# Two reorderings on TensorE and a split of the first loads over two issuing engines, in a two-layer decoder kernel

## The reference

```python
x = _layernorm(x + _L0_attn_ref(x, W_in, b_in, W_out, b_out))       # block A
x = _layernorm(x + _L0_xattn_ref(x, ctx_2048, W_fc, ..., W_v, b_v)) # block B
x = _layernorm(x + _L0_ffn_ref(x, ...))                             # block C: 64 experts
...                                                                 # blocks D, E, F: layer 1
# A, for each sequence and 16 heads of 16 features, causal:
weights = softmax(q @ k.T * 0.25 + mask); attn = weights @ v; out = attn @ W_out.T + b_out
# B: sup = relu(ctx @ W_fc.T + b_fc); ref = relu(x @ W_fc.T + b_fc)
# q from ref, k from sup, weights = softmax(q @ k.T * 0.25); result = ref + (weights @ sup) by W_v + b_v
```

## Time and profile before

| what | us |
|---|---|
| median of three runs | 1002.47 |
| lowest and highest | 1000.71, 1004.54 |
| the profiled execution's own time | 1001.67 |
| its span, first to last instruction | 999.9 |
| first matmul | 6.23 |
| one step of the pipeline in A, 51.17 to 60.50 | 9.33 |
| one step in B, 132.46 to 142.37 | 9.91 |

### The profile page before, as it was taken

The page is one execution under the profiler, slowest core; times in us unless marked ns, Lnnn a source line. Parts: engine busy times, 40 slices in busy tenths (PEclk is TensorE's granted clock), DMA queues, the critical chain, the costliest instruction groups (busy, mean ns, idle before and its releaser), DMA issues. The chain is left out here.

```text
span 999.9 us, 18709 instructions
## 1 busy us (share of the span) xinstructions
PE 955.7 (96%) x6121; PEld 755.5 (76%) x6121; DVE 636.5 (64%) x1474; ACT 443.4 (44%) x862; POOL 313.3 (31%) x514
## 2 busy tenths in 40 slices
PE   6999999999999999999999999998999998999994
PEld 4788887687888888888887855667787775888883
DVE  3676777655555555555556666778778865555555
ACT  3777786432332233222222223426776784323321
POOL 1133123244444444444445303210000106344430
PEclk9999999999999999999999999999999999999998
DMA  8000000256433333333333000011111121554501
GB/s 289 13 17 18 2 2 1 51 158 184 142 130 127 111 111 110 111 113 111 111 112 103 21 1 10 1 37 40 27 36 35 34 67 23 127 152 110 113 18 42
DMA packets 37423, 75.55 MB, mean 76 GB/s; under 512 B 7121, under 2 KB 18365, under 8 KB 37222
## 3 DMA queue, kind: packets, MB, share of 16 engines
q1 hardware_dynamic: 37074, 74.53, 25.9%
q0 software_dynamic: 288, 0.23, 0.2%
HBM read 67.57 MB, written 2.40 MB: 70 GB/s over the span
## 5 line engine op out<-in xcount | busy, mean ns | idle before, releaser
L1054 PE MATMUL ps<-shared 128*128 128x512 f32 x1560 | 378.0, 391 | 1.0 <-POOL shared L2105 0.9
L1054 PEld LDWEIGHTS ps<-shared 128*128 128x128 f32 x1560 | 292.0, 188 | 66.6 <-issue 5.1
L1477 ACT ACTIVATE shared<-pT 128x512 fp32r<-128x512 f32 x130 | 82.4, 634 | 287.9 <-DVE pT L1903 287.8
L2103 POOL CAST shared<-wraw 128x512 fp32r<-128x512 f32 (+1 forms) x130 | 91.9, 707 | 295.0 <-PE ps L1080 274.2
L1906 DVE TENSOR_TENSOR al<-pT,shared 128x512 fp32r<-128x512 f32 x130 | 120.8, 929 | 91.0 <-ACT shared L1477 91.0
L1895 DVE TENSOR_TENSOR e<-e,ps 128x512 f32<-128x512 f32 x130 | 89.4, 688 | 122.3 <-PE ps L1054 119.7
L1080 PE MATMUL ps<-shared 128*128 128x512 f32 x520 | 161.9, 392 | 0.3 <-DVE al L1906 0.2
L2105 POOL TENSOR_TENSOR shared<-wraw,shared 128x512 fp32r<-128x512 f32 (+1 forms) x130 | 133.9, 1030 | 10.4
L1080 PEld LDWEIGHTS ps<-shared 128*128 128x128 f32 x520 | 97.4, 188 | 22.5 <-DVE al L1906 1.2
L1471 ACT ACTIVATE e<-ps 128x512 f32<-128x512 f32 x130 | 77.8, 598 | 76.8 <-PE ps L1054 76.8
L1903 DVE TENSOR_TENSOR pT<-e,kbd 128x512 f32<-128x512 f32 x130 | 101.0, 777 | 7.1
(11 more groups left out here) (228 smaller groups left out, 1381.7 us busy)
## 6 DMA issues: line engine op xcount, KB each, us to landing
kbd<-combine_C SPq DMA_DIRECT2D x46, 512.0 KB
wraw<-in_C_w SPq DMA_DIRECT2D x48, 384.0 KB, 8.5
kbd<-combine_F SPq DMA_DIRECT2D x15, 512.0 KB
wraw<-in_F_w SPq DMA_DIRECT2D x17, 384.0 KB, 6.9
kbd<-kbd SPq DMA_DIRECT2D x96, 32.0 KB, 1.9
kT<-kbd SPq DMA_DIRECT2D x48, 32.0 KB, 1.8
c_ctx_t<-in_ctx_t SPq DMA_DIRECT2D x1, 1024.0 KB, 8.8
out<-c_x_rows SPq DMA_DIRECT2D x2, 512.0 KB, 2.9
```

Source lines behind the costliest of these rows:

```text
L1054: mm = pe.matmul(GU[t][s], w[u][:, (c * 2 + s) * P:(c * 2 + s + 1) * P], xx[:, c, t * HALF:(t + 1) * HALF], start=(i == 0), stop=(i == 5))
L1477: act.activation(ah[t][:, :], a2[t], ACT.Copy).then_inc(S("ah"), 1)
L2103: pool.tensor_copy(wh[u][:, lo:hi], wraw[k][:, lo:hi]).then_inc(S("m_wh"), 1)
```

## The change

Three edits. In TensorE's pipeline `ref_rows(t-4)` moves ahead of `project_keys(t-1)`, and `second_transposes(t-2, 1)` moves ahead of `out_T(t-3)`. Of the loads of groups A0, A1 and A2 the nine small ones (tensors with fewer than 256 elements in a row, and the two biases `bv` and `bo` of 256) are issued by ScalarE at its start; SyncE issues the six others, in the old order, and then goes on as before.

```diff
+        SECOND = [t for g in ("A0", "A1", "A2") for t, src in loads[g] if np.prod(src.shape[1:]) < D]
+        SECOND += [W["A", "bv"], W["A", "bo"]]
+
+        def first_loads(eng, queue):
+            for group in ("A0", "A1", "A2"):
+                for t, src in loads[group]:
+                    if queue == any(t is x for x in SECOND):
+                        eng.dma_start(t[tuple(slice(None) for _ in t.shape)], src).then_inc(S(f"{group}_loaded"), 16)
...
-            for group in ("A0", "A1", "A2", "A3"):
-                load_weights(group)
+            first_loads(sp, 0)
+            load_weights("A3")
...
             for t in range(2 * B + 5):
+                if ly == "B":
+                    ref_rows(t - 4)
                 if lp:
                     project_keys(t - 1)
                 if ly == "A":
                     out_project(t - 4)
-                if ly == "B":
-                    ref_rows(t - 4)
...
                 if lx:
                     x_T(t - 5)
+                if lv:
+                    second_transposes(t - 2, 1)
                 if lo == "A":
                     out_T(t - 3)
-                if lv:
-                    second_transposes(t - 2, 1)
...
+            first_loads(act, 1)
             loaded(act, "A0")
```

## The result

The changed kernel took 1005.46 us (median of 15 runs, 1004.72 to 1009.28), the kernel before 1003.6 beside it (15 runs, the three shown ahead of the prediction among them). The ratio is 1.0032, 95% interval 1.0023 to 1.0041, which is 3.2 us of 1003. The means differ by 3.0 us. The two medians differ by only 1.9, because eight of the fifteen runs before lie between 1003.6 and 1004.5 and the others are spread down to 999.4. I count the change as slower by about 3.2 us: a difference clear of the noise, inside the 0.5% that the prediction called "same", and 0.5 us above the upper end of its range.

The account below looks back on a forecast made before the run. TensorE, busy 96%, was taken to bound the kernel. Loads -1.2, `ref_rows` +1.4 and `out_T` 0 turned the profiled 1001.67 into 1001.9 us, or the median 1002.47 into 1002.7, range 1000.6 to 1005.0.

Parts of the forecast that it names:

- What bounds the kernel: Whole span: TensorE, busy 96%, sets the end; its waits are at the start and at the steps in B.
- Part 2: Steps 12 to 16, `ref_rows` ahead of the keys: each 0.26 to 0.33 us longer, +1.4 us taken.
- Part 1: First loads split over SyncE and ScalarE: the start and all behind it 1.2 us earlier.
- A0 is complete at 5.0, which is 1.2 us earlier: Start: `wk` lands at 4.6 and `bk` at 5.0, so the first matmul leaves 6.23 by 1.2 us.
- A2 and the later groups are also issued earlier [...] No one behind them waits longer than before: Loads behind the first group: SyncE saves nine issues, some 4 us, and no later reader waits longer.
- The bound that the long rows might end at a fixed moment: First matmuls: if TensorE's long rows end at a fixed moment, up to 0.6 us of the gain is lost.
- The table load: ScalarE's start: wanted at 7.2 instead of 8.38, with its nine issues done by 5.2, a cover of 2 us.
- The third rival: Start: ScalarE still issuing loads when the first keys are ready; +3.5 us, +4.9 in all, 1007.4; chance 0.05.
- The first rival: Start gains nothing, by interleaving or another last transfer; +1.4 us in all, 1003.9; chance 0.17.
- Part 3: Steps 3 to 10, `out_T` behind the last transposes: same work in another order, cost 0.
- The cover that I named: Steps 3 to 10: ScalarE's 0.21 us idle and about 0.1 overlap absorb a 0.3 us delay; without it 0.8.
- The sum: Whole kernel: -1.2 + 1.4 + 0 on the profiled 1001.67 gives 1001.9; the median becomes 1002.7.

Follow-up runs that it names:

- part 2 alone: Kernel before with only `ref_rows` moved ahead of the keys, run twice (x2, x11): ratios 1.0020 and 1.0023.
- x8: Kernel before with the small first loads split to ScalarE, except `bo`, which SyncE issues ahead of `wo`: 1000.6 us, ratio 0.9991.
- x10: Kernel before with the load split, `bo` still last on ScalarE but in its own semaphore group awaited only by its reader: 1003.2 us, ratio 1.0003.
- x1: Kernel before with only the split of the first loads over SyncE and ScalarE: 1004.5 us, ratio 1.0013.
- x17: Kernel before with only the split of the first loads, second time: 1003.4 us, ratio 1.0014.
- x2: Kernel before with only `ref_rows` moved ahead of the keys: 1004.5 us, ratio 1.0020.
- x11: Kernel before with only `ref_rows` moved ahead of the keys, second time: 1004.2 us, ratio 1.0023.
- x3: Kernel before with only `out_T` moved behind the last transposes: 1001.9 us, ratio 1.0000.
- x12: Kernel before with three extra transposes, results overwritten, in each of steps 12 to 16: 1004.3 us, ratio 1.0026.
- x13: Kernel before with six extra transposes, results overwritten, in each of steps 12 to 16: 1006.0 us, ratio 1.0038.
- x0: Unchanged copy of the kernel before: 1001.5 us, ratio 0.9989.
- x9: Changed kernel with all three edits, but `bo` issued by SyncE: 1004.3 us, ratio 1.0019.
- x4: Kernel before with the load split and the `out_T` move, without the `ref_rows` move: 1005.2 us, ratio 1.0036, six runs.
- x5: The changed kernel with all three edits, run again: 1004.9 us, ratio 1.0039.
- after: The changed kernel with all three edits, in its first measurement and profile: 1005.46 us, ratio 1.0032.
- x15: Kernel before with the load split and the `ref_rows` move, without the `out_T` move: 1005.6 us, ratio 1.0035.
- x14: Kernel before with the `ref_rows` move and three extra transposes in each of steps 12 to 16: 1005.5 us, ratio 1.0028.

## Why the prediction was wrong, point by point

**What bounds the kernel** was right: nearly all that mattered was on TensorE at the two places that the rows had shown, with 0.28 us more at 602.6.

**Part 2 was right, step by step.** The copy into `XT` ends at 112.38, the weight load of `ref_rows` starts 0.10 us later, the keys 0.17 behind it and the values 1.10 behind these, nearly as forecast. A step takes 122.69 - 112.48 = 10.21 against 9.91, so +0.30, and the five make 1.46 to 1.49, against 1.4. The time of part 2 alone came out above that, at 2.0 and 2.3 us. See below.

**Part 1 failed, and it is the step that made the prediction wrong.** Of its terms:

- *"A0 is complete at 5.0, which is 1.2 us earlier"*: mis-sized, and mostly because of its starting point. The 6.23 of the earlier trace rows is the latest first matmul of nine profiles in which SyncE issues all; the others are 5.43 to 6.04, the mean 5.81. With the split (eleven profiles) it is 5.31 to 6.10, the mean 5.64. The gain is 0.2 us, not 1.2. `bk` came as forecast: 1.16 + 3.5 = 4.7. But `wk`, which I had landing at 4.6 by its old 3.0 us, takes 3.6 to 4.4 beside the transfers that ScalarE starts, where it takes 2.5 to 3.0 when SyncE issues all, and now it ends the wait.
- *"A2 and the later groups are also issued earlier [...] No one behind them waits longer than before"*: wrong. I looked at the issues and not at what they collide with. SyncE has six issues instead of fifteen ahead of A3, so A3's 768 KB transfers go out from 4.14 us instead of 8.42 and are under way together with ScalarE's small ones. `bo`, the last of these, lands at 4.82 + 8.1 = 12.9. Before, it was issued at 7.47 and took 3.0: 10.5. It is issued 2.65 us earlier and lands 2.4 us later. All of A2 counts for whoever waits for it, so the first scores start 0.05 to 0.63 us later behind the first matmul than in the kernel before. That the bulk makes `bo` late, and not ScalarE's queue as such, is argued from x8, where SyncE issues it ahead of the bulk and it takes 5.2; no run held the bulk back with `bo` last on ScalarE. It can't be the whole of it: the identity on ScalarE still takes 6.2 us in x8.
- The bound that the long rows might end at a fixed moment: in the nine unsplit profiles the clock's first rise came at 9.25 to 16.02 us of the span, which is 3.7 to 10.0 us behind the first matmul. It is fixed neither in the span nor behind the start, so what a start 0.2 us earlier gives back to it can't be read from one profile.
- The table load was not late (7.89, forecast 7.2; before 8.38), and ScalarE was through with its issues at 5.65 (forecast 5.2). The third rival is out: its issues took 0.39 to 0.94 us each.

Together: after step 2 the ledgers of the eight profiles with `bo` last on ScalarE stand at +0.1 in the mean, those of the nine unsplit ones at -0.7 and those of x8 to x10 at -0.6. So by the ledgers the split costs 0.8 us by then instead of gaining 1.2, and another 0.28 us at 602.6; 1.1 to 1.3 us is what the times of x1 and x17 say. Without the wait for `bo` the times of the split are those of the kernel before (x8, x10). The 0.8 holds the wait of 0.3 us and the later clock, and four of the eight profiles make it.

The first rival had the transfers interleave and the start gain nothing. It was the nearest, but it stopped at zero and could not become a loss. The Trainium skill (DMA: Bandwidth & Descriptors, section "Issuing engines are not separate DMA queues") says that transfers of several issuing engines interleave on the same DMA engines. The landing times of `bo` (8.1 against 3.0) and of the identity (6.7 against 2.2) agree, and go further than the zero that I had worked out from it.

**Part 3**: forecast 0, measured 1.0000 in time and about +0.2 us in the ledgers, 0.03 in each step. The cover that I named nearly holds.

**The sum** was -1.2 + 1.4 + 0 = +0.2. By the experiments it is +1.2 (x1, x17) + 2.1 (x2, x11) + 0 (x3) = +3.3, against 3.2 measured. 2.4 us of the miss are part 1 and 0.7 part 2. Each of these terms is uncertain by some 1 us, so how well the sum closes is in part luck.

**What stays open** is the 0.5 to 0.9 us by which part 2, and x12 and x13, cost more than their ledgers across the five steps, if it is more than noise. The clock is the only thing in the traces that I found to hold them: mean 0.9912 and 0.9919 in x2 and x11, where the kernel before had 0.9925 and 0.9929 beside them. An estimate supports it. One slope fitted to all executions of x0 to x17 and of the kernel before beside them gives 0.62 us for each 0.001 of mean clock; at equal clock x2 and x11 are then 1.2 and 1.7 us above the kernel before, 1.45 in the mean, against 1.47 in the ledgers. It is rough: it leaves 1.9 for x12 (ledger 1.64) and 4.0 for x13 (3.27), and puts x0 at -1.0. The stretch at C is a candidate for the lower clock. It isn't a matter of how late C starts, since it is there at 182.4 and 183.6 and absent at 182.8, 183.6 and 184.4 (x2, x9; x4, x13, x5). But take how far C's first matmul is behind the clock's first rise in the same execution. In five profiles this is 168.3 to 168.9 us (after, x2, x9, x11, x15), and all five have the stretch. Of the other fifteen fourteen have none, at 165.8 to 168.1 or at 169.5 and above; x17, at 164.9, has one and doesn't fit (its first rise, at 18.09 us, is the latest of all twenty). Of the ten profiles without part 2 or more work eight lie at 164.9 to 167.4. So a delay of 1.5 us would push many executions into those 168.3 to 168.9, and one of 3.1 us beyond them, as x14's did (169.5). That fits all but one profile, but it was read from them after they had run, and no run tested it.

No version beats the kernel before: x8 is the best at 0.9991, with an interval that holds 1.

## What to carry to other kernels

When loads are split over two issuing engines, don't only count issue time. Ask what the relieved queue will send next, and whether it is large: a small transfer issued late beside it lands later than it did in the old single queue, and every reader of its semaphore group waits, not only its own. Here the late `bo` held up TensorE, which never reads it. Issue the small transfers that somebody needs first ahead of the bulk on either queue, or give the late one a semaphore of its own.

Don't take the start of one execution as the start of the kernel. The load that decided mine was 0.4 us later in that profile than in the mean of nine, a third of the gain that I forecast.

## What the runs showed of the hardware that I had not expected

- A 128 KB transfer took 3.0 us from issue to landing in one queue among its peers, 5.1 to 5.2 as one of SyncE's in the split and 7.8 to 8.4 as ScalarE's last, with 2.5 MB of SyncE's loads beside it. A 64 KB one took 2.2 and 6.7.
- In nine profiles of kernels that are the same up to there, the first matmul started at 5.43 to 6.23 us of the span, and the clock rose to 2.4 GHz for the first time at 9.25 to 16.02 us. In the two with the earliest rise (9.25 and 10.25) the execution is 1.8 us ahead by 19 us.
- An engine that is 96% busy over the span still has stretches of 3.4 or 6.8 us at 1.2 GHz in the middle of the kernel, which in the ledgers make 0.5 to 1.9 and 2.4 to 3.5 us each. Whether one comes behind a hole changes between executions, and nine more matmuls in two such holes did not raise the mean clock (0.9923 against 0.9931 in the kernel before, 0.9929 against 0.9934 in the changed one).
- Eight or nine issues ahead of ScalarE's first operation came with a delay of 0.27 to 0.28 us on TensorE far behind them, at 91.5 us with eight and at 602.6 with nine, in all eleven kernels that have them. The cause is not shown.
